# Two-head full attention: four batches in a loop against four batches in one pipeline

## The chip, the cores and the metric

The kernel runs on one core of one Trainium2 chip. The metric is the device time of one execution in microseconds. A core has a matrix engine (TensorE, PE in the profile; its weight loads are PEld), three engines for elementwise work (VectorE or DVE, ScalarE or ACT, GpSimd or POOL) and a queue for transfers (SyncE or SP). Each engine runs its own list of instructions in order; they wait for each other by semaphores. TensorE writes only to PSUM, eight banks of 512 f32 columns on 128 partitions (`ps[:, bank, :]`); GpSimd reads and writes SBUF alone.

## The reference, cut to what matters

The model has two layers over x of 4 batches x 512 rows x 128 columns in f32. Its parts in order: linear attention, windowed attention with a feed-forward part, small-head attention, windowed attention again, small-head mixing, a mixture of experts, then the part that is changed, and a second mixture of experts. The changed part is

```python
x = x + attn_b(_layernorm(x))             # eps 1e-5, no gain

def attn_b(x, ln_gamma, ln_beta, q_gamma, k_gamma, w_q, w_k, w_v, w_o, b_o):
    xn = layernorm(x, ln_gamma, ln_beta)  # a second norm, eps 1e-5
    q, k, v = (heads(xn @ w.T) for w in (w_q, w_k, w_v))   # 2 heads of 64
    qn = rmsnorm(q, q_gamma) * 64 ** -0.5
    kn = rmsnorm(k, k_gamma)
    attn = softmax(einsum('bhid,bhjd->bhij', qn, kn))      # 512 x 512, no mask
    out = merge(einsum('bhij,bhjd->bhid', attn, v))
    return out @ w_o.T + b_o
```

So each row is normed twice in a row, and each head's output goes through its half of the output weights.

## The kernel before, in words

`program` writes one list of instructions for each engine, in eight stages. Between stages every engine drains and counts up `batch_done`; SyncE waits for four of them, clears the semaphores (`clear`, L2109) and counts up `batch_go`, for which all engines wait. The stream x stays in SBUF as `X` (128 partitions x 16 row tiles x 128). The stages up to the fourth are written out in full; the fifth and the seventh are loops (`Fori`).

The seventh stage is `full_attention`, four times, once for each batch (`Fori(0, NB)`, L901, L1275, L1856, L2085). VectorE copies the batch's four row tiles from `X` to `XB` (L1860) and makes two layer norms one after the other (`layer_norm`, L1310): statistics of each tile (L1312), their aggregation (L1315), adding eps (L1317); GpSimd raises to the power -0.5 (`root`, L1879, which also does the 16 columns of q and k later); VectorE subtracts and multiplies (L1320). TensorE turns the result (`transposes`, L318), ScalarE applies gain and offset on the way to `xT` (L1177), and TensorE projects q, k and v: twelve products (L751). Matmuls in f32 appear in the profile as two instructions each, transposes as one. ScalarE squares q and k (L1180) and copies v (L918, the helper for all plain copies); VectorE sums the squares (L1715) and scales (L1716), GpSimd takes the power, VectorE multiplies q and k by it (L1722). TensorE turns both (L318), ScalarE and VectorE copy them out with their gains (L1184, L1725).

Then come four steps, one for each tile of 128 query rows, with both heads in each:

- `scores` (TensorE, L766): 128 x 512 scores for each head, into banks 0 and 1 or 2 and 3 in turn;
- `maxima` (VectorE, L1734 and L1735): the row maximum of both heads, times the negative scale;
- `exps` (ScalarE, L1195): the exponential of each head, with its row sum;
- `turn` (TensorE, L777): eight transposes of the probabilities, into banks 4 and 5;
- the copies out: ScalarE bank 4 (L918), VectorE bank 5 (L1743);
- `values` (TensorE, L786): probabilities times v, eight products of 64 columns, into bank 6.

TensorE's order is scores(0), scores(1), then for each step turn(st), scores(st + 2), values(st). After the fourth step VectorE takes the reciprocal of the sums (L1749) and multiplies (L1750), TensorE turns the result (L318) and multiplies by the output weights (L801), ScalarE copying between, and VectorE adds it and the bias to `XB` (L1754, L1755) and copies back to `X` (L1862). A drain of all engines (`stage_done`, L298) and the hand-over by SyncE end a batch. The eighth stage is `experts(1)`; it begins with the statistics of all 16 tiles of `X`, and in its main loop adds with fused multiply-adds from PSUM (L1805).

Of the kernel before, what the change touches and what calls it, by code (L numbers as in the profile page):

```python
# [111 lines left out]
def program(nc, x_in, w_in, c_in, r_in, out, scratch, c_at):  # L112
# [3 lines left out]
    with ExitStack() as ctx:  # L116
# [35 lines left out]
        def carve(n):  # L152
# [71 lines left out]
        m_qT = carve(512)  # L224
        m_kT = carve(512)
        m_v = carve(512).rearrange("p (j n) -> p j n", j=NT)
        m_p = carve(2048).rearrange("p (z h s) -> p z h s", z=2, h=2)
        m_pT = carve(1024).rearrange("p (h j t) -> p h j t", h=2, j=NT)
        m_os = carve(512)
        m_oT = carve(512)  # L230
        m_sq = carve(1024)
        m_qk = carve(1024).rearrange("p (j n) -> p j n", j=NT)
        m_rs = sb("m_rs", [P, NT * 2])
# [21 lines left out]
            m_xT_ps m_xT m_proj m_sq m_qk_in m_tps m_kT_in m_qv_in m_s m_max m_exp m_tp m_pT_a m_pT_b m_pv  # L255
            m_os_in m_oT_ps m_oT_in m_out""".split()
# [56 lines left out]
        def _(pe):  # L313
# [431 lines left out]
            def full_attention(ln):  # L745
                pe.wait_ge(s.ln_out, ln)
                transposes(0, lambda j: Y[:, j, :]).then_inc(s.m_xT_ps, 1)
                pe.wait_ge(s.m_xT, 1)
                for j in range(NT):
                    for c in range(3):  # L750
                        last = mm(ps[:, 1 + c, j * P:(j + 1) * P], xT[:, j * P:(j + 1) * P],  # L751
                                  W("d_qkv", 128 * c, 128 * c + 128), start=True, stop=True)
                last.then_inc(s.m_proj, 1)
                pe.wait_ge(s.m_qk_in, 1)
                transposes(4, lambda j: m_qk[:, j, 0:128])
                transposes(5, lambda j: m_qk[:, j, 128:256]).then_inc(s.m_tps, 1)
                pe.wait_ge(s.m_qv_in, 1)
                pe.wait_ge(s.m_kT_in, 1)
                steps, dv = full_steps(), DF

                def scores(st):
                    if st >= 2:
                        pe.wait_ge(s.m_exp, st - 1)
                    i, hs = steps[st]
                    for hh, (h, rows) in enumerate(hs):
                        last = mm(ps[:, 2 * (st % 2) + hh, :], m_qT[rows, i * P:(i + 1) * P], m_kT[rows, :],  # L766
                                  start=True, stop=True)
                    last.then_inc(s.m_s, 1)

                def turn(st):  # L770
                    pe.wait_ge(s.m_exp, st + 1)
                    if st:
                        pe.wait_ge(s.m_pT_a, st)
                        pe.wait_ge(s.m_pT_b, st)
                    for hh in range(2):
                        for j in range(NT):
                            last = tr(ps[:, 4 + hh, j * P:(j + 1) * P], m_p[:, st % 2, hh, j * P:(j + 1) * P], ident)  # L777
                    last.then_inc(s.m_tp, 1)

                def values(st):  # L780
                    pe.wait_ge(s.m_pT_a, st + 1)
                    pe.wait_ge(s.m_pT_b, st + 1)
                    i, hs = steps[st]
                    for hh, (h, _) in enumerate(hs):
# [5 lines left out]
                scores(0)  # L790
                scores(1)
                for st in range(len(steps)):
                    turn(st)
                    if st + 2 < len(steps):
                        scores(st + 2)
                    values(st)
                pe.wait_ge(s.m_os_in, 1)
                transposes(0, lambda j: m_os[:, j * P:(j + 1) * P]).then_inc(s.m_oT_ps, 1)
                pe.wait_ge(s.m_oT_in, 1)
                for j in range(NT):  # L800
                    last = mm(ps[:, 1, j * P:(j + 1) * P], m_oT[:, j * P:(j + 1) * P], W("d_wo"), start=True, stop=True)  # L801
                last.then_inc(s.m_out, 1)
# [57 lines left out]
            def stages(which):  # L860
                ln = 0
                for i, st in enumerate(which):
                    if st == "c":
                        ln += 1
                        head_attention(ln)
                    else:
                        ln += 2
                        full_attention(ln)
                    stage_done(pe, i + 1)
# [30 lines left out]
            if STAGES >= 7:  # L900
                with pe.Fori(0, NB) as b:  # L901
                    pe.wait_ge(batch_go, b + NP + 6)
                    pe.sem_inc(batch_seen, 1)
                    stages(["d"])
                    pe.drain().then_inc(batch_done, 1)
            if STAGES >= 8:
                pe.wait_ge(batch_go, NB + NP + 6)
# [7 lines left out]
        def _(act):  # L915
# [259 lines left out]
            def full_attention():  # L1175
                act.wait_ge(s.m_xT_ps, 1)
# [1148 lines left out]
```

## Time and profile before

| | us |
|---|---|
| median of 3 runs | 2269.24 |
| the runs | 2269.24, 2271.3, 2257.24 |
| profiled execution, its own time | 2261.32 |
| its span | 2259.5 |
| TensorE busy (share of the span) | 1630.8 (72%) |
| TensorE weight loads | 1160.5 (51%) |
| VectorE busy | 1318.2 (58%) |
| ScalarE busy | 1083.2 (48%) |
| GpSimd busy | 874.8 (39%) |
| mean granted clock of TensorE | 0.846 |

The span is the stretch that the profile covers, from the first instruction to the last; the execution's own time is 1.8 us longer. Busy shares are means over eight stages. Records give a start, a duration and what ended the idle time before; neighbouring matmuls overlap in their records, so what a group costs is read from start to start. A granted clock of 1.00 is 2.4 GHz, of 0.50 1.2 GHz.

### The profile page before, as it was taken

Reading aid. Unit: us, or ns where it says so; the run is one execution under the profiler, and the core shown is the slowest. Engines: PE = TensorE matmul, PEld = TensorE weight load, DVE = VectorE, ACT = ScalarE, POOL = GpSimd, SP = SyncE. Lnnn points to the kernel's source line nnn. Section 1 sums busy time; section 2 is a strip of 40 time slices with the busy share of each in tenths; the row PEclk is TensorE's granted clock in tenths of the full one; section 3 lists DMA queues with packets and bytes.
Section 4 is the critical chain, followed back from the end, with each engine's and each line's share of the span. In section 5 each row is a group of like instructions: output and inputs, shape, how many; then the busy total and the mean of one; then the engine's idle time right before and its main releaser. Section 6 shows DMA issues by size and latency. Waiting matters only on the chain. (4 is left out here: it accounts for less than half of the span.)

```text
span 2259.5 us, 37774 instructions
## 1 busy us (share of the span) xinstructions
PE 1630.8 (72%) x13344; PEld 1160.5 (51%) x13344; DVE 1318.2 (58%) x3740; ACT 1083.2 (48%) x2727; POOL 874.8 (39%) x628
## 2 busy tenths in 40 slices
PE   6999996889988568988868998884011166455586
PEld 5888883666666333445436666662010055344464
DVE  3454545886776245567568777752968745433344
ACT  3565664877787245654347778762000022222132
POOL 1232234766665013244366666640544402100102
PEclk9999998999999868998779999997555578777578
DMA  4000000111111000000001111100000001000001
GB/s 178 1 1 1 1 1 12 30 27 24 28 30 22 6 0 1 1 1 2 1 20 27 27 26 29 24 20 5 0 0 0 0 1 38 0 0 0 0 4 53
DMA packets 31073, 36.43 MB, mean 16 GB/s; under 512 B 19120, under 2 KB 21168, under 8 KB 30512
## 3 DMA queue, kind: packets, MB, share of 16 engines
q1 hardware_dynamic: 29872, 32.01, 5.4%
q8 instruction: 106, 1.74, 0.3%
q0 software_dynamic: 1024, 2.10, 0.3%
q14 instruction: 71, 0.58, 0.1%
HBM read 12.08 MB, written 3.15 MB: 7 GB/s over the span
## 5 line engine op out<-in xcount | busy, mean ns | idle before, releaser
L918 ACT ACTIVATE arena<-ps 128x512 f32<-128x512 f32 (+5 forms) x684 | 373.8, 606 | 297.9 <-PE ps L318 143.1
L318 PE MATMUL ps<-consts,arena 128*128 128x128 f32 x416 | 89.1, 362 | 296.4 <-DVEq L1695 139.8
L318 PEld LDWEIGHTS ps<-consts,arena 128*128 128x128 f32 x416 | 61.1, 181 | 328.1 <-DVEq L1695 141.6
L1053 ACT ACTIVATE arena<-arena,g_small 128x128 f32<-128x128 f32 x512 | 199.0, 404 | 0.5
L1153 ACT ACTIVATE arena<-ps 128x320 f32<-128x320 f32 (+4 forms) x256 | 132.5, 561 | 137.4 <-PE ps L676 134.6
L1460 DVE CUSTOM_DVE_ANT_0 arena<-ps,consts,g_ss 128x128 f32<-128x128 f32 x512 | 145.6, 347 | 77.1 <-PE ps L482 72.2
L1962 POOL TENSOR_TENSOR arena<-arena,consts 128x512 f32<-128x512 f32 (+1 forms) x64 | 92.9, 1452 | 194.3 <-ACT arena L1153 194.2
L1983 POOL TENSOR_TENSOR arena<-arena 128x512 f32<-128x512 f32 x64 | 82.1, 1282 | 183.8 <-DVE arena L1468 183.7
L2036 POOL TENSOR_TENSOR arena<-arena 128x2048 f32<-128x2048 f32 x16 | 109.5, 6842 | 99.9 <-DVE arena L1687 99.9
L676 PE MATMUL ps<-arena 32*128 32x160 f32 (+4 forms) x1024 | 119.9, 454 | 21.1 <-ACT arena L1153 10.5
L1879 POOL TENSOR_TENSOR rstd<-rstd,consts 128x4 f32<-128x4 f32 (+2 forms) x16 | 28.8, 1798 | 262.4 <-DVE rstd L1317 219.9
L1467 DVE TENSOR_TENSOR arena<-ps,tabs 128x512 f32<-128x512 f32 x128 | 87.7, 685 | 50.7 <-ACT arena L1022 44.8
L1993 POOL TENSOR_TENSOR g_ss<-g_ss,consts 128x8 f32<-128x8 f32 x64 | 105.4, 1647 | 7.1
L1805 DVE SCALAR_TENSOR_TENSOR arena<-ps,arena 128x128 f32<-128x128 f32 x256 | 72.1, 344 | 61.8 <-PE ps L850 60.3
L1402 DVE TENSOR_REDUCE arena<-arena 128x8 f32<-128x1032 f32 x32 | 39.3, 1228 | 115.7 <-ACT arena L976 115.7
L583 PE MATMUL ps<-arena,weights 128*128 128x512 f32 (+1 forms) x192 | 101.4, 639 | 6.0 <-ACT arena L1082 4.1
L676 PEld LDWEIGHTS ps<-arena 32*128 32x128 f32 x1024 | 60.8, 204 | 87.4 <-ACT arena L1153 53.9
L1996 POOL TENSOR_TENSOR g_ss<-g_ss,consts 128x8 f32<-128x8 f32 x64 | 104.7, 1636 | 0.0
L1053 ACT ACTIVATION_READ_ACCUMULATOR arena<-arena,g_small 128x1 f32 x512 | 103.8, 203 | 0.0
L1909 POOL TENSOR_TENSOR arena<-arena,consts 128x8 f32<-128x8 f32 x32 | 52.6, 1645 | 124.2 <-DVE arena L1402 124.2
L2052 POOL DMA_INDIRECT sorted_rows<-arena,e_idx x32 | 30.9, 967 | 169.6 <-DVE arena L1805 162.3
L1986 POOL TENSOR_TENSOR arena<-arena 128x512 f32<-128x512 f32 x64 | 81.4, 1271 | 38.8 <-issue 35.2
(249 smaller groups left out, 4287.2 us busy)
## 6 DMA issues: line engine op xcount, KB each, us to landing
arena<-arena SPq DMA_DIRECT2D x112, 128.0 KB, 2.3
weights<-in_w SPq DMA_DIRECT2D x1, 5069.0 KB, 24.0
weights<-in_w SPq DMA_DIRECT2D x1, 2052.0 KB, 12.5
arena<-Y SPq DMA_DIRECT2D x16, 128.0 KB
arena<-Y SPq DMA_DIRECT2D x16, 127.0 KB
consts<-in_c SPq DMA_DIRECT2D x1, 1278.0 KB, 8.6
out<-X SPq DMA_DIRECT2D x1, 1024.0 KB, 5.1
sorted_rows<-arena,e_idx POOLq DMA_INDIRECT x32
```

What stands on the lines that cost most here:

```text
L318: last = tr(ps[:, bank, j * P:(j + 1) * P], src(j), ident)
L583: mm(ps[0:m, 4 + c % 2, :], W("f_w1", at, at + m), g_hnT, start=True, stop=True)\
L676: last = mm(ps[:, 2 * (st % 2) + hh, 0:n], b_kT[rows, k % 2, r, j * P:(j + 1) * P], b_qT[rows, k % 2, j * P:j * P + n], start=True, stop=True)
L918: copy = lambda o, i: act.activation(o, i, ACT.Copy)
L1053: last = act.activation(g_p[:, n % 2, 4 * hf + i, :], g_sc[:, 4 * hf + i, :], ACT.Exp, scale=-1.0, bias=g_mn[:, h:h + 1], accum_out=g_rs[: ...
L1153: act.activation(b_p[:, U % 2, 2 * gp:2 * gp + 2, at:at + n], ps[:, b:b + 2, 0:n], ACT.Exp, scale=float(HD) ** -0.5).then_inc(s.b_exp, 1)
L1460: last = dve.tensor_tensor_reduce(g_sc[:, 4 * hf + i, :], ps[:, 4 + hf, i * P:(i + 1) * P], C("mask_f" if n % NT else "mask_f0"), g_ss[:, ...
L1467: tt(heads(low[0]), heads(src), table(tabs_at), ALU.mult)
L1962: pool.tensor_tensor(v, v, m.unsqueeze(1).broadcast_to([P, NG, n]), ALU.mult)\
L1993: stepped_after(pool.tensor_tensor(ss[:, 8:16], ss[:, 8:16], C("neghalf", 0, 8), ALU.pow))
L1996: pool.tensor_tensor(ss[:, 0:8], ss[:, 0:8], C("neghalf", 0, 8), ALU.pow).then_inc(gs.root, 1)
L2036: pool.tensor_tensor(c_mix[:, u % 2].rearrange("p (h d t) -> p h d t", h=HB, t=HB), c_e[:, u % 2].unsqueeze(2).broadcast_to(full), vals.un ...
```

## The change

The loop over batches goes; `full_attention` is called once and covers all 16 row tiles. On each engine one loop over a step number t runs from -6 or -4 to 15 or 16. At step t the rows of tile t are worked on, and between them lies one piece of the preparation of a later batch, chosen by (t + 4) % 4 (and (t + 6) % 4 for the norm). `rows_at(t)` is true for t from 0 to 15.

- The two norms are one: the root is taken of v * (1 + eps) + eps * eps instead of v + eps (`norm_var(k, twice)`), and the result goes to `Y` for all batches. The copies between `X` and `XB` go.
- The weights of value and output are multiplied on the chip once at the start (`fold_weights`: one transpose, a copy, a product for each head, a copy). A head's values are then x times a 128 x 128 matrix (`m_w`), so that probabilities times values gives 128 columns for each head, already through the output weights. The output projection with its transposes and copy goes. VectorE adds each head to the stream with a fused multiply-add, scaled by the reciprocal of the head's sum (`add_rows`), and GpSimd adds the bias to `X` (`m_xb`).
- Scores have banks 0 and 1 alone, turned probabilities 2 and 3, values 4, q and k 5 and 6, transposes of x and values 7. The turned x, q, k, the values, the probabilities and the turned probabilities in SBUF have two buffers each.

The core of the diff:

```diff
+            def full_attention():            # TensorE
+
+                def turn_x(z):
+                    pe.wait_ge(gs.ln, 4 * NB + z + 1)
+                    need(pe, s.m_vin, 2 * z)
+                    transposes(7, lambda j: Y[:, NT * z + j, :]).then_inc(s.m_xT_ps, 1)
...
+                def scores(n):
+                    z, i = n // NT, n % NT
+                    pe.wait_ge(s.m_qT, z + 1)
+                    pe.wait_ge(s.m_kT, z + 1)
+                    need(pe, s.m_exp, n)
...
+                def turn_probs(n):
+                    pe.wait_ge(s.m_exp, n + 1)
+                    need(pe, s.m_pT_a, n)
+                    need(pe, s.m_pT_b, n)
...
+                def values(n):
+                    z = n // NT
+                    pe.wait_ge(s.m_pT_a, n + 1)
+                    pe.wait_ge(s.m_pT_b, n + 1)
+                    pe.wait_ge(s.m_vin, 2 * z + 2)
+                    need(pe, s.m_out, n)
+                    for h in range(2):
                         for j in range(NT):
-                            last = mm(ps[:, 6, i * P + h * dv:i * P + (h + 1) * dv], m_pT[:, hh, j, :],
-                                      m_v[:, j, h * dv:(h + 1) * dv], start=j == 0, stop=j == NT - 1)
+                            last = mm(ps[:, 4, h * P:(h + 1) * P], m_pT[:, n % 2, h, j, :], m_v[:, z % 2, h, j, :],
+                                      start=j == 0, stop=j == NT - 1)
...
+                fold_weights()
+                for t in range(-4, TT + 1):
+                    if rows_at(t):
+                        scores(t)
+                    if rows_at(t - 1):
+                        values(t - 1)
+                    z, r = (t + 4) // NT, (t + 4) % NT
+                    if z < NB:
+                        if r == 0:
+                            turn_x(z)
+                        elif r == 1:
+                            project_qk(z)
+                        elif r == 2:
+                            project_v(z, 0)
+                        else:
+                            turn_qk(z)
+                            project_v(z, 1)
+                    if rows_at(t):
+                        turn_probs(t)
```

ScalarE's loop has, in this order at each step, the exponentials of t, the piece (copy of turned x; squares; copy of the first head's values; copies of q and of the second head's values), and the copy of probabilities of head 0. VectorE's loop:

```diff
+                for t in range(-6, TT + 1):
+                    if rows_at(t):
+                        maxima(t)
+                    z, r = (t + 6) // NT, (t + 6) % NT
+                    if z < NB and r == 0:
+                        norm_stats(0, stream(z))
+                        norm_var(0, True)
+                    if z < NB and r == 1:
+                        norm_apply(0, Y[:, NT * z:NT * z + NT, :], stream(z), gs.ln)
+                    z, r = (t + 4) // NT, (t + 4) % NT
+                    if 0 <= z < NB and r == 2:
+                        sums(z)
+                    if rows_at(t - 1):
+                        add_rows(t - 1)
+                    if 0 <= z < NB and r == 2:
+                        normalise(z)
+                    if 0 <= z < NB and r == 3:
+                        keep_k(z)
+                    if rows_at(t):
+                        keep_probs(t)
```

where `sums(z)` reduces the squares and asks GpSimd for the power of 16 columns, `normalise(z)` waits for it and multiplies q and k (two products from PSUM), and `add_rows` is

```diff
+                    dve.wait_ge(s.m_pv, n + 1)
+                    dve.wait_ge(s.m_xb, n // NT + 1)
+                    after(dve.reciprocal(r, r))
+                    stt(x, ps[:, 4, 0:P], r[:, 0:1], x, ALU.mult, ALU.add).then_inc(s.m_half, 1)
+                    dve.wait_ge(s.m_half, n + 1)
+                    stt(x, ps[:, 4, P:2 * P], r[:, 1:2], x, ALU.mult, ALU.add).then_inc(s.m_out, 1)
```

GpSimd's loop has the root of the norm at (t + 6) % 4 == 0, the bias at (t + 6) % 4 == 2, and the power for q and k at (t + 4) % 4 == 2, in this order. The hand-over by SyncE after the stage is kept, once instead of four times.

## Rows read from the trace of the kernel before

**Rows 1.** Windows: from:to, length, busy (instructions) by engine, clock, DMA.

```profile
0.00:1566.20 1566.20, 1322.58 (x11736) 928.22 (x11736) 942.48 (x2917) 956.74 (x2512) 705.61 (x564) 0.92 0.08 20
...
1919.30:1970.70 51.40, 27.26 (x160) 21.07 (x160) 19.98 (x49) 11.42 (x25) 4.95 (x3) 0.73 0.00 0
...
2073.50:2134.80 61.30, 37.24 (x160) 29.10 (x160) 19.88 (x49) 11.53 (x25) 4.91 (x3) 0.58 0.00 0
...
2104.50:2124.90 20.40, 19.52 (x80) 15.57 (x78) 4.70 (x7) 4.56 (x11) 0.00 (x0) 0.50 0.00 0
1950.40:1960.90 10.50, 9.62 (x73) 7.73 (x74) 4.86 (x7) 4.63 (x13) 0.00 (x0) 1.00 0.01 2
```

**Rows 2.** Timeline, first batch ahead of the scores: start, us, instruction, idle before.

```profile
1919.87 0.87 DVE L1312 BATCH_NORM_STATS2 stats<-XB 128x6 f32<-128x128 f32 x4
...
1921.45 1.04 POOL L1879 TENSOR_TENSOR rstd<-rstd,consts 128x4 f32<-128x4 f32 x1 [12.34 <-DVE rstd L1317]
...
1923.67 0.87 DVE L1312 BATCH_NORM_STATS2 stats<-Y 128x6 f32<-128x128 f32 x4
...
1927.46 1.12 PE L318 MATMUL ps<-consts,Y 128*128 128x128 f32 x4 [24.71 <-DVE Y L1320]
...
1929.45 4.97 PE L751 MATMUL ps<-weights,xT 128*128 128x128 f32 x24 [0.87 <-ACT xT L1177]
...
1935.51 1.22 DVE L1715 TENSOR_REDUCE rstd<-arena 128x16 f32<-128x1024 f32 x1 [8.10 <-ACT arena L1180]
...
1939.95 1.29 DVE L1722 TENSOR_TENSOR arena<-ps,rstd 128x512 f32<-128x512 f32 x2 [3.01 <-POOL rstd L1879]
...
1941.29 1.97 PE L318 MATMUL ps<-consts,arena 128*128 128x128 f32 x8 [6.88 <-DVE arena L1722]
...
1944.19 3.54 PE L766 MATMUL ps<-arena 64*128 64x512 f32 x8 [0.94 <-DVE arena L1725]
```

**Rows 3.** Timeline, first batch, its row tiles.

```profile
1947.77 0.69 ACT L1195 ACTIVATE arena<-ps,small 128x512 f32<-128x512 f32 x1 [3.79 <-DVE small L1735]
...
1949.27 1.09 PE L777 MATMUL ps<-consts,arena 128*128 128x128 f32 x8 [1.54 <-ACT arena L1195]
...
1950.30 1.13 PE L766 MATMUL ps<-arena 64*128 64x512 f32 x4
...
1951.36 2.00 PE L786 MATMUL ps<-arena 128*128 128x64 f32 x16
1951.47 1.22 DVE L1734 TENSOR_REDUCE small<-ps 128x2 f32<-128x1024 f32 x1 [0.38 <-PE ps L766]
...
1952.93 0.69 ACT L1195 ACTIVATE arena<-ps,small 128x512 f32<-128x512 f32 x1 [1.77 <-DVE small L1735]
...
1953.19 1.04 PE L777 MATMUL ps<-consts,arena 128*128 128x128 f32 x8
...
1958.14 0.69 DVE L1743 COPY arena<-ps 128x512 f32<-128x512 f32 x1 [1.37 <-PE ps L777]
...
1958.98 1.97 PE L786 MATMUL ps<-arena 128*128 128x64 f32 x16 [0.88 <-DVE arena L1743]
```

**Rows 4.** Timeline, ends of batches: reciprocal, next batch's copy, last copy back.

```profile
1964.71 0.20 DVE L1749 RECIPROCAL m_rs<-m_rs 128x8 f32<-128x8 f32 x1 [2.15 <-PE ps L786]
...
1970.85 0.43 DVE L1860 TENSOR_SCALAR XB<-X 128x512 f32 x1 [0.43 <-SPq L2111]
...
2134.36 0.43 DVE L1862 TENSOR_SCALAR X<-XB 128x512 f32 x1
```

**Rows 5.** Timeline, fourth batch, a step.

```profile
2111.44 2.08 PE L766 MATMUL ps<-arena 64*128 64x512 f32 x4
...
2113.45 3.67 PE L786 MATMUL ps<-arena 128*128 128x64 f32 x16
...
2116.92 1.91 PE L777 MATMUL ps<-consts,arena 128*128 128x128 f32 x8
```

**Rows 6.** Line L1805 by itself: engine, operation, durations in ns, starts, forms.

```profile
L1805 DVE SCALAR_TENSOR_TENSOR arena<-ps,arena x256: 340/343/352, 1849.3 to 2238.6; 128x128 f32<-128x128 f32 x128
```

More of the change, by code:

```diff
@@ L767, in scores @@
                                   start=True, stop=True)
                     last.then_inc(s.m_s, 1)
[L770 to L775, printed above, removed]
+                def turn_probs(n):
+                    pe.wait_ge(s.m_exp, n + 1)
+                    need(pe, s.m_pT_a, n)
+                    need(pe, s.m_pT_b, n)
+                    for h in range(2):
@@ L776, in turn @@
                         for j in range(NT):
-                            last = tr(ps[:, 4 + hh, j * P:(j + 1) * P], m_p[:, st % 2, hh, j * P:(j + 1) * P], ident)
+                            last = tr(ps[:, 2 + h, j * P:(j + 1) * P], m_p[:, n % 2, h, j * P:(j + 1) * P], ident)
                     last.then_inc(s.m_tp, 1)
[L780 to L784, printed above, removed]
+                def values(n):
[4 more added lines that the diff above has]
+                    need(pe, s.m_out, n)
+                    for h in range(2):
@@ L791, in full_attention @@
[L791 to L801, printed above, removed]
@@ L900, in _ @@
             if STAGES >= 7:
[L901 to L905, printed above, removed]
+                pe.wait_ge(batch_go, NP + 6)
+                pe.sem_inc(batch_seen, 1)
+                full_attention()
+                pe.drain().then_inc(batch_done, 1)
             if STAGES >= 8:
-                pe.wait_ge(batch_go, NB + NP + 6)
+                pe.wait_ge(batch_go, NP + 7)
                 pe.sem_inc(batch_seen, 1)
@@ new lines, in exps @@
+                def exps(n):
+                    c = 2 * (n % 2)
+                    act.wait_ge(s.m_max, n + 1)
+                    need(act, s.m_tp, n - 1)
+                    need(act, s.m_out, n - 1)
+                    for h in range(2):
+                        last = act.activation(m_p[:, n % 2, h, :], ps[:, h, :], ACT.Exp, bias=nma[:, c + h:c + h + 1],
+                                              scale=scale, accum_out=m_rs[:, n % 2, h:h + 1])
+                    last.then_inc(s.m_exp, 1)
@@ new lines, in keep_probs @@
+                def keep_probs(n):
+                    act.wait_ge(s.m_tp, n + 1)
+                    need(act, s.m_pv, n - 1)
+                    copy(m_pT[:, n % 2, 0], ps[:, 2, :].rearrange("p (j t) -> p j t", j=NT)).then_inc(s.m_pT_a, 1)
+                act.wait_ge(s.m_wv_ps, 1)
+                copy(m_wv, ps[:, 7, 0:P]).then_inc(s.m_wv, 1)
+                act.wait_ge(s.m_w_ps, 1)
+                copy(m_w, ps[:, 5:7, 0:P]).then_inc(s.m_w, 1)
+                for t in range(-4, TT):
+                    if rows_at(t):
+                        exps(t)
+                    z, r = (t + 4) // NT, (t + 4) % NT
+                    if z < NB:
+                        if r == 0:
+                            keep_x(z)
+                        elif r == 1:
+                            squares(z)
+                        elif r == 2:
+                            keep_values(z, 0)
+                        else:
+                            keep_q(z)
+                            keep_values(z, 1)
+                    if rows_at(t):
+                        keep_probs(t)
@@ L1336, in norm_var @@
                 after(last, True)
-                ts(g_rstd[:, k, :], mv[:, NT * k:NT * k + NT, 1], EPS5, None, ALU.add).then_inc(gs.var, 1)
+                v = mv[:, NT * k:NT * k + NT, 1]
+                if twice:
+                    ts(g_rstd[:, k, :], v, 1.0 + EPS5, EPS5 * EPS5, ALU.mult, ALU.add).then_inc(gs.var, 1)
+                else:
+                    ts(g_rstd[:, k, :], v, EPS5, None, ALU.add).then_inc(gs.var, 1)
                 rooted.next()
@@ L2251, in small_at, with rows_at @@
     return sum(small_width(glob, i) for i in range(j))
-def full_steps():
-    return [(i, [(h, slice(64 * h, 64 * h + 64)) for h in range(2)]) for i in range(NT)]
+def rows_at(n):
+    return 0 <= n < TT
 def kernel(**inputs):
```

272 lines of the change are left out of this document (129 added, 143 removed).

## The prediction

> **What bounds the stage now.** I read the page first (busy shares, the 40 slices, the costliest groups), then the table of windows by stage, then the timeline of one batch. The page spreads the span over eight stages with different limits, so its shares say little here; the change touches only the seventh stage, the two-head attention of the second layer, which the windows place at 1919.4 to 2134.8 us: four batches, one after the other, 51.4 us each in the first three and 61.3 in the fourth [rows 1]. In each of the first three TensorE is busy 27.3 of 51.4 us, VectorE 20, ScalarE 11.4: nobody is full, so the stage is a chain of hand-overs. In the timeline it falls in three parts. Ahead of the scores: two layer norms, projections, q and k normalised, from 1919.41 (the copy L1860, which like that of 1970.85 takes 0.43 us, 0.46 with its hand-over, ahead of the statistics at 1919.87) to 1944.19, where the scores L766 begin: 24.8 us, nearly serial [rows 2, 4]. Then four row tiles, 1944.2 to 1964.71: 20.5 us, where TensorE becomes the bound: one warm step is scores 1.06, values 1.83 and eight transposes 0.98 us, start to start (1950.30, 1951.36, 1953.19), 3.87 together [rows 3]. Then a tail of 6.1 us from the reciprocal (1964.71) to the next batch's copy (1970.85) [rows 4]. The fourth batch costs 9.9 us more with the same instructions: from 2104.5 to 2124.9 TensorE works 19.5 of 20.4 us at a granted clock of 0.50 (1.2 GHz), where a stretch of steps in the first batch had 1.00 (2.4 GHz) [rows 1]. There scores take 2.01, values 3.47 and transposes 1.91: 7.4 us a step [rows 5].
>
> **The stage after, part by part.** Everything is counted from 1919.41, when VectorE may begin.
>
> *Ahead of the first scores.* The copy to XB goes (0.46). One norm instead of two: 1919.87 to 1923.67, 3.80 us; the second (another 3.79 up to 1927.46) goes [rows 2]. Transposes and ScalarE's copy, 1927.46 to 1929.45: 1.99. Query and key projection is 16 of the 24 matmuls of L751: 16/24 of 4.97 is 3.31. From the end of L751 (1934.42) to the reduce at 1935.51: 1.09; from the reduce over the scaling and GpSimd's power of 16 columns to the product at 1939.95: 4.44 (VectorE idle for 3.01 of it); the product to the transposes: 1.34; eight transposes 1.97 [rows 2]. Then PE makes the second head's values (8 instructions at 4.97/24 = 0.207: 1.66) before the scores, while k is scaled. Sum with 0.06 for a hand-over: 19.7 us, where the first batch has 24.8. It is paid once instead of four times: the others' preparation lies in the steps.
>
> *A plain step.* Banks 0 and 1 are the only score banks now, and the PE list of step t is scores(t), values(t-1), a piece of the next batch, transposes(t). The scores of the next step stand behind transposes that wait for both exponentials. So, unlike now, a step is a closed ring: scores to maximum 1.17 (1950.30 to 1951.47), maximum and its scaling to the exponential 1.46 (to 1952.93), two exponentials to the transposes 1.50 (1947.77 to 1949.27), transposes to scores 1.03 (to 1950.30) [rows 3]: 5.16 us. That is longer than the 3.87 of today: this part of the change speaks against it, and costs 16 x 1.29 = 21 us, which the hidden preparation has to earn back. VectorE's adding of rows lies in the ring: a reciprocal, about 0.24, and two fused multiply-adds of 0.343 [rows 4, 6], with hand-overs make 1.02, starting at 2.9 when values end, done by 3.9, ahead of the copy of probabilities at 5.16.
>
> *Steps with a piece.* PE's own sum decides where it passes the ring. Step with transposes of x: 1.06 + 1.83 + 0.5 + 1.0 = 4.4, hidden: 5.16. With the query and key projection (16 matmuls, as values: 1.83): 1.06 + 1.83 + 1.83 + 1.0 = 5.72. With eight transposes of q, k and eight matmuls: 1.2 + 1.83 + 0.95 + 0.92 + 1.0 = 5.9. The fourth kind, with the first head's values, is where VectorE stops everything. Its list there: maximum (done at 1.17 + 1.46 = 2.63), statistics and variance of the norm after (1919.87 to 1921.45: 1.58, so 4.21), sums, add the rows, then the product, which waits for GpSimd's power (4.44 after the sums begin, so 8.65; the rows go into the 3.01 that VectorE idles in it) and takes 1.34 (9.99); only behind it the copy of probabilities (0.69 and a hand-over, 10.72) and the next maximum [rows 2, 3]. A maximum normally starts at 1.17, so this step is 9.55 us; the third such step has no norm any more, 7.97. Queued behind that wait are the copy, so values(t), and the next maximum, so both exponentials: nobody else can fill it.
>
> *Sum of the steps.* Twice 5.16 + 5.72 + 9.55 + 5.9 = 26.33; once 24.75; four plain ones 20.64: 98.05 us. The end after the last transposes: copy 0.84 (1958.14, where the values started at 1958.98), values 1.97 and the rows 1.02: 3.85.
>
> *The clock.* In the long step PE idles from about 6.1 to 10.75, some 4.6 us, and then has cold prices if the clock falls. The rows bound this from both sides: idle stretches of under 1 us between steps keep 1.00 [rows 1, 3], and after the long gaps ahead of the scores the transposes ran at 0.50 (1.97 for eight, not 1.04) [rows 2, 3]. A step of the last kind costs 5.2 us more when all of it is cold (11.1, below, against 5.9); nothing lost is the other end. I take 2.2 for each of three, and 1.5 for the first step, which starts cold: 8 us (0 to 15).
>
> *Edits at nothing.* The product of value and output weights (one transpose, a copy, four matmuls, a copy, 2.3 us by the rows for x) lies under the first norm (3.80), and would cost those 2.3 without it. Values widen from 64 to 128 columns: the same 16 instructions, and cold ones of 128 columns took 0.207 each, those of 64 columns 3.67/16 = 0.229 [rows 2, 5], so width is free; if it doubled the warm 1.83, PE's sum would be 5.7 instead of 5.16 and the stage some 15 us longer; I take 0. The bias moves to GpSimd (idle there); the output projection, its transposes, the division, two adds and the copy back (the 6.1 us tail) go three times outright [rows 4], and the three loop ends in it with them.
>
> **Sum.** 19.7 + 98.05 + 3.85 + 8 = 129.6 us against 215.4 (1919.41 to 2134.79, the end of the last copy back [rows 4]): 85.8 us less. The profiled execution has a span of 2259.5 and a time of 2261.32, so 2175.5 on it. Its time is below the median of the runs (2269.24; 2257.24 to 2271.3); the mean of all four is 2264.8, 3.4 above, so I say **2179 us**. The other stages keep their instructions; their clock may fall differently, a few us either way. A measurement tells about 1% (some 23 us) from no change.
>
> A page rule that speaks against this: the trace shows the eight transposes warm at 1.04 us inside a stretch at 1.00 [rows 1, 3]. The Trainium skill, "TensorE: Matmul & The Clock Gate", Part 4: PE-mode transpose, says that transposes don't count as busy for the clock as matmuls do. By it the gap of the long step is longer for the gate by the transposes in it and all three following steps would be wholly cold (5.2 instead of 2.2 each, 2188 us). No row here separates the two kinds.
>
> **Rivals.**
> (A) *The clock stays at 1.2 GHz through most of the stage*, as in most of the fourth batch, where full work at 0.50 went on for 20 us [rows 1]. The steps are then 2.01 + 3.47 + 1.91 = 7.4 plain, 8.4, 10.8, 9.55 and 11.1 with pieces: 3 x 39.85 + 4 x 7.4 less 0.5 = 148.6; with 19.7 and 6 at the end 174.3, so 41 us less than now: 2224. For it: that row, and the gaps every four steps. Against: three batches in four got 1.00, and a step now has twice the columns in its values and project work between.
> (B) *The long step isn't long*, because the power or the norm costs less in company; then PE's sums set all steps. That takes off 12.8 us of stall and 6.6 of clock: 2160. Against: all in that chain has been taken from rows, and VectorE's list is in order.
> (C) *Slower than now: code supply.* The loop over batches goes and the same work is written out four times. If each PE instruction then had to wait for its code, the stage passes today's 215.4 once 86 us are lost over some 650 PE instructions, 0.13 us each, more than an instruction's own 0.115: a step of some 10.5 us instead of 5.2 to 6. At 0.15 us each it is 97 us: 2276. Against: the first 1566 us are written out likewise and run 11736 matmuls, 7.5 a us, with TensorE busy 1322 us [rows 1]; this stage needs about 5.
> (D) *The change doesn't do what it says*: an unforeseen wait makes batches follow one another again. Four times 19.7 ahead, steps 16 x 5.16, tails of 3: 173, 42 less: 2223. The waits allow batch z+1 to be prepared while z is worked (two buffers each), so little speaks for it.
>
> **Chances.** Forecast 0.77 (its own range 2162 to 2198), A 0.12, B 0.05, D 0.03, C 0.03. The range of 8 in 10 goes from 2160 (B's value, and no clock loss from the fastest run) to 2212 (part of A, or the doubled width and a cold start after each gap). Faster by over 1%: all but C and a rest, 0.96; within 1% 0.01; slower by over 1% 0.03.
>
> **What would show it.** Right: the stage takes 125 to 135 us; the first scores begin 20 us after its start, and the maxima of steps 4 to 16 are about 5.2, 5.7, 9.5 and 5.9 us apart in turn, and 5.2 in the last four; in the long ones VectorE's product waits for the power some 2 us, and TensorE has a gap of 4 to 5 us; the clock shows one dip after each. GpSimd's two kinds of powers and four adds keep their durations. Wrong: plain steps at 7.4 (A), values at over 3 us in a stretch at 1.00 (width), PE gaps put down to issue (C), or no scores while the next batch is projected (D).

## The result, and the profile after

The changed kernel takes 2175.15 us (median of four runs, 2173.67 to 2177.07), the kernel before 2270.27 in the same comparison (2257.24 to 2275.85): a ratio of 0.9601, 95% interval 0.9572 to 0.963, so it is faster by 95 us between the medians and by 4.0% by the ratio. The prediction said 2179, with a range of 2160 to 2212. The profiled execution of the changed kernel takes 2174.38 us with a span of 2172.2; the prediction's sum for a profiled execution was 2175.5. The runs also lie closer together: 3.4 us from lowest to highest, where the kernel before has 18.6. One execution of all those told below, one of the kernel of experiment 2, took 2955.68 us at a mean granted clock of 0.545, and its median and ratio leave it out.

The page of the changed kernel begins:

```profile
span 2172.2 us, 37710 instructions
...
PE 1611.1 (74%) x13333; PEld 1148.2 (53%) x13333; DVE 1305.1 (60%) x3712; ACT 1084.7 (50%) x2729; POOL 875.8 (40%) x628
```

Busy time hardly moved on any engine (TensorE 20 us less, VectorE 13, ScalarE and GpSimd about 1 more). So most of the 87.3 us that the span lost, 68 of them on TensorE, are idle time: nearly the same work now lies side by side. The stage as a window (from:to, length, busy by engine, clock), and its last four steps:

```profile
1920.90:2047.50 126.60, 96.98 (x629) 77.66 (x629) 69.39 (x168) 47.20 (x102) 20.07 (x12) 0.88 0.00 1
2022.90:2047.50 24.60, 18.62 (x129) 13.92 (x128) 13.38 (x28) 8.77 (x21) 0.00 (x0) 1.00 0.00 1
```

TensorE is busy 97 of 126.6 us, where it was 27.3 of 51.4 in a batch [rows 1]; the granted clock is 0.88 on the average of the stage, where batches had 0.73 and 0.58.

The length of the stage is read between two instructions of VectorE: from the end of the update of X by the experts, just ahead of it, to the next stage's first statistics. These are the two of the kernel before, then the two of the changed kernel:

```profile
1916.60 2.29 DVE L1809 TENSOR_TENSOR X<-X,arena 128x2048 f32<-128x2048 f32 x1 [12.50 <-DMA arena<-sorted_rows]
...
2135.13 3.19 DVE L1312 BATCH_NORM_STATS2 stats<-X 128x6 f32<-128x128 f32 x16 [0.34 <-SPq L2111]
```

```profile
1918.22 2.29 DVE L1882 TENSOR_TENSOR X<-X,arena 128x2048 f32<-128x2048 f32 x1 [12.87 <-DMA arena<-sorted_rows]
...
2048.16 3.19 DVE L1360 BATCH_NORM_STATS2 stats<-X 128x6 f32<-128x128 f32 x16 [0.72 <-SPq L2191]
```

The stage had 216.2 us and has 127.6: 88.6 less. The six earlier stages have the same instructions, yet reach this point 1.6 us later (1920.5 against 1918.9), and the last stage is 0.3 shorter: 88.6 - 1.6 + 0.3 = 87.3. These two remainders come and go: in the kernels below, whose first 1900 us are all the same code, the stage began anywhere from 1915.4 to 1926.6. So each experiment is read by the length of its stage first and by its median second.

Ahead of the scores, the timeline of the changed kernel, answering to [rows 2] (start, duration, instruction):

```profile
1920.90 0.87 DVE L1376 BATCH_NORM_STATS2 stats<-X 128x6 f32<-128x128 f32 x4 [0.38 <-SPq L2191]
...
1922.56 0.38 ACT L945 ACTIVATE arena<-ps 128x256 f32<-128x256 f32 x1 [0.90 <-PE ps L752]
...
1924.72 1.11 PE L318 MATMUL ps<-consts,Y 128*128 128x128 f32 x4 [2.21 <-DVE Y L1395]
...
1926.70 3.78 PE L767 MATMUL ps<-weights,arena 128*128 128x128 f32 x16 [0.87 <-ACT arena L1208]
...
1931.58 1.22 DVE L1769 TENSOR_REDUCE m_rn<-arena 128x16 f32<-128x1024 f32 x1 [5.52 <-ACT arena L1214]
...
1936.02 1.29 DVE L1777 TENSOR_TENSOR arena<-ps,m_rn 128x512 f32<-128x512 f32 x2 [3.01 <-POOL m_rn L2126]
...
1940.97 1.51 PE L790 MATMUL ps<-arena 64*128 64x512 f32 x4
```

Statistics to transposes is 3.82 (predicted 3.80), the sums to the product 4.44 (4.44), and the first scores begin 20.07 us after the start (19.7). The second line is the last copy of the multiplied weights: over at 1922.94, 1.8 us before TensorE has its first transposes to do, so hidden as said.

A plain step and the long one, answering to [rows 3]. First the end of a plain step of the last batch, in the same timeline:

```profile
2033.22 1.13 PE L790 MATMUL ps<-arena 64*128 64x512 f32 x4
...
2034.28 2.05 PE L811 MATMUL ps<-arena 128*128 128x128 f32 x16
2034.39 1.23 DVE L1790 TENSOR_REDUCE small<-ps 128x2 f32<-128x1024 f32 x1 [0.38 <-PE ps L790]
...
2035.86 0.69 ACT L1233 ACTIVATE arena<-ps,small 128x512 f32<-128x512 f32 x1 [1.94 <-DVE small L1791]
...
2037.36 1.09 PE L800 MATMUL ps<-consts,arena 128*128 128x128 f32 x8 [1.03 <-ACT arena L1233]
2038.38 1.13 PE L790 MATMUL ps<-arena 64*128 64x512 f32 x4
```

Scores at 2033.22 and at 2038.38: 5.16 us, the ring to the hundredth, and TensorE waits 1.03 of it for the exponentials. The values (L811, now 128 columns wide) take 2.05, where those of 64 columns took 2.00 [rows 3]: the width costs next to nothing here. Then the first long step, VectorE's list and TensorE behind it:

```profile
1954.86 1.23 DVE L1790 TENSOR_REDUCE small<-ps 128x2 f32<-128x1024 f32 x1 [0.38 <-PE ps L790]
...
1956.19 0.86 DVE L1376 BATCH_NORM_STATS2 stats<-X 128x6 f32<-128x128 f32 x4
...
1957.58 1.22 DVE L1769 TENSOR_REDUCE m_rn<-arena 128x16 f32<-128x1024 f32 x1
...
1959.09 2.90 POOL L2126 TENSOR_TENSOR m_rn<-m_rn,consts 128x16 f32<-128x16 f32 x1 [0.32 <-DVE m_rn L1770]
...
1962.02 1.29 DVE L1777 TENSOR_TENSOR arena<-ps,m_rn 128x512 f32<-128x512 f32 x2 [2.17 <-POOL m_rn L2126]
1963.23 0.68 DVE L1796 COPY arena<-ps 128x512 f32<-128x512 f32 x1
1963.83 1.21 DVE L1790 TENSOR_REDUCE small<-ps 128x2 f32<-128x1024 f32 x1
...
1964.01 3.75 PE L811 MATMUL ps<-arena 128*128 128x128 f32 x16 [4.04 <-DVE arena L1796]
```

Maximum to maximum is 8.97; VectorE stands 2.17 us before the product, and the copy behind it keeps TensorE idle for 4.04. When TensorE resumes, the same values take 3.75 instead of 2.05: the clock has fallen. Two windows around that gap and after it show when:

```profile
1958.80:1962.90 4.10, 1.17 (x6) 0.30 (x4) 1.82 (x7) 0.60 (x1) 2.90 (x1) 0.92 0.00 0
1962.90:1969.70 6.80, 5.69 (x29) 5.72 (x30) 4.51 (x12) 2.13 (x5) 1.09 (x1) 0.54 0.00 0
...
1997.00:2047.40 50.40, 41.13 (x299) 32.10 (x297) 28.73 (x58) 20.85 (x47) 2.91 (x1) 1.00 0.00 1
```

### The profile page after: what moved, and what is told of

It reads as the page before. It is cut to its first block and busy times, and to the rows that moved or that the text cites. A ratio compares the mean times of both kernels' runs of the same rounds, so it can differ in the third digit from the quotient of the medians.

```text
span 2172.2 us, 37710 instructions
## 1 busy us (share of the span) xinstructions
PE 1611.1 (74%) x13333; PEld 1148.2 (53%) x13333; DVE 1305.1 (60%) x3712; ACT 1084.7 (50%) x2729; POOL 875.8 (40%) x628
## 5 line engine op out<-in xcount | busy, mean ns | idle before, releaser
L945 ACT ACTIVATE arena<-ps 128x512 f32<-128x512 f32 (+4 forms) x686 | 374.4, 605 | 296.8 <-PE ps L318 126.3
L318 PE MATMUL ps<-consts,arena 128*128 128x128 f32 x400 | 84.4, 358 | 265.9 <-DVEq L1747 139.8
L1454 DVE TENSOR_REDUCE arena<-arena 128x8 f32<-128x1032 f32 x32 | 39.3, 1228 | 115.8 <-ACT arena L1003 115.8
L689 PE MATMUL ps<-arena 128*32 128x160 f32 (+4 forms) x1024 | 87.4, 415 | 4.7 <-issue 4.7
```

The lines of the kernel that those rows point to most:

```text
L318: last = tr(ps[:, bank, j * P:(j + 1) * P], src(j), ident)
L945: copy = lambda o, i: act.activation(o, i, ACT.Copy)
```

## The experiments

The starts of the 16 maxima (L1790, or its line in each kernel) are the ruler: the time between them is the length of a step. Each kernel here has one trace, only the changed one has two, so how far the stage of the kernel before moves from one execution to the next isn't known; a few us of its 216.2 could be of that kind.

**1. The norms alone** (label norm), on the kernel before:

```diff
-                layer_norm(XB[:, 0:NT, :], Y[:, 0:NT, :], NT, EPS5).then_inc(s.ln_out, 1)
-                dve.wait_ge(s.ln_out, 1)
-                layer_norm(Y[:, 0:NT, :], Y[:, 0:NT, :], NT, EPS5).then_inc(s.ln_out, 1)
+                layer_norm(XB[:, 0:NT, :], Y[:, 0:NT, :], NT, EPS5, True).then_inc(s.ln_out, 1)
...
+                if twice:
+                    root(n, ts(rstd[:, 0:n], mv[:, 0:n, 1], 1.0 + EPS5, EPS5 * EPS5, ALU.mult, ALU.add))
```

> The kernel before with one part of the change alone: the two norms made as one, loop over batches and all else as before. If the norms are serial at the head of each batch (the working of the prediction), each of the four batches is shorter by 3.79 us, the stretch from the second statistics to the first transposes: 15 us less, some 2251 to 2256. Rival, that the head was covered by something else: no difference. Second rival, the clock: a batch that starts at another moment may run its row tiles warm or cold, 10 us either way for a batch, as the fourth batch of the kernel before showed.

Measured: 2238.82 against 2257.66 of the kernel before on that chip, ratio 0.9913 (0.9885 to 0.9942). The stage takes 195.4 us, 20.8 less. The batches start

```profile
1915.88 0.43 DVE L1861 TENSOR_SCALAR XB<-X 128x512 f32 x1 [0.52 <-SPq L2111]
...
1963.56 0.43 DVE L1861 TENSOR_SCALAR XB<-X 128x512 f32 x1 [0.43 <-SPq L2111]
...
2011.23 0.43 DVE L1861 TENSOR_SCALAR XB<-X 128x512 f32 x1 [0.45 <-SPq L2111]
...
2060.34 0.43 DVE L1861 TENSOR_SCALAR XB<-X 128x512 f32 x1 [0.44 <-SPq L2111]
```

so the first two take 47.68 and 47.67, 3.8 less than the 51.4 before, as the serial head demands. The third takes 49.1 and the fourth, to the next stage's statistics at 2110.81, 50.5. In the third the row tiles are as long as in the second, and what is longer is the tail behind them, which ran at half the clock. The tails of the second and of the third batch, as windows:

```profile
2005.30:2010.40 5.10, 1.81 (x12) 1.39 (x12) 2.29 (x5) 0.60 (x1) 0.00 (x0) 0.83 0.00 0
2053.00:2059.50 6.50, 3.19 (x12) 2.50 (x12) 2.30 (x5) 0.60 (x1) 0.00 (x0) 0.50 0.00 0
```

The fourth has such a tail too, and its row tiles at 0.79 where the second batch has 0.91, but not the long stretch at 0.50 that made the fourth batch of the kernel before 61.4 us. Serial norms account for 15.2 us; of the 5.6 beyond, the fourth batch gives 7.2 and the third takes back 1.5, both where the granted clock differs.

**2. The weights alone** (fold), on the kernel before, with both norms; the product of the weights is made anew in each batch:

```diff
+                tr(ps[:, 7, 0:P], W("d_qkv", 2 * P, 3 * P), ident).then_inc(s.m_wv_ps, 1)
+                pe.wait_ge(s.m_wv, 1)
+                for h in range(2):
+                    rows = slice(DF * h, DF * h + DF)
+                    last = mm(ps[:, 5 + h, 0:P], m_wv[rows, :], W("d_wo")[rows, :], start=True, stop=True)
...
-                            last = mm(ps[:, 6, i * P + h * dv:i * P + (h + 1) * dv], m_pT[:, hh, j, :],
-                                      m_v[:, j, h * dv:(h + 1) * dv], start=j == 0, stop=j == NT - 1)
+                            last = mm(ps[:, 6 + st % 2, h * P:(h + 1) * P], m_pT[:, h, j, :], m_v[:, h, j, :],
+                                      start=j == 0, stop=j == NT - 1)
...
-                transposes(0, lambda j: m_os[:, j * P:(j + 1) * P]).then_inc(s.m_oT_ps, 1)
```

> The kernel before with the other part alone: value and output weights multiplied on the chip, at the head of each batch under the norms, a head's values 128 columns wide, no division, turning and output projection behind the row tiles, the rows added head by head in the steps, the bias added under the projections; loop over batches and both norms as before. By the rows the tail from the reciprocal to the copy back (5.28 us in the first batch) becomes 1.02, and eight of the 24 projecting matmuls go off the head (1.66): 5.9 us for each batch, 24 in all, some 2242 to 2248. If a product of 128 columns cost twice one of 64, the values would add 1.83 us in each of 16 steps, 29 us, and the kernel would be no faster than before. If the weights' product were not covered, 2.3 us for each batch come back, 9 in all.

Measured: 2231.93 against the same 2257.66, ratio 0.9891 (0.9853 to 0.9929); the stage takes 190.6 us, 25.6 less. The tail, answering to [rows 4]:

```profile
1960.44 0.17 DVE L1753 RECIPROCAL m_rs<-m_rs 128x2 f32<-128x2 f32 x1 [1.32 <-PE ps L798]
1960.64 0.35 DVE L1754 SCALAR_TENSOR_TENSOR XB<-ps,m_rs,XB 128x128 f32<-128x128 f32 x1
1961.03 0.35 DVE L1755 SCALAR_TENSOR_TENSOR XB<-ps,m_rs,XB 128x128 f32<-128x128 f32 x1
1961.52 0.43 DVE L1877 TENSOR_SCALAR X<-XB 128x512 f32 x1
...
1962.38 0.43 DVE L1875 TENSOR_SCALAR XB<-X 128x512 f32 x1 [0.43 <-SPq L2126]
```

From the reciprocal to the copy back is 1.08 us, where it was 5.28 (1964.71 to 1969.99). The wide products cost next to nothing, and their rival of 29 us falls. The 24 us that were expected came out near, but not as four times 5.9. The batches begin

```profile
1916.23 0.43 DVE L1875 TENSOR_SCALAR XB<-X 128x512 f32 x1 [0.52 <-SPq L2126]
...
1962.38 0.43 DVE L1875 TENSOR_SCALAR XB<-X 128x512 f32 x1 [0.43 <-SPq L2126]
...
2010.52 0.43 DVE L1875 TENSOR_SCALAR XB<-X 128x512 f32 x1 [0.45 <-SPq L2126]
...
2058.53 0.43 DVE L1875 TENSOR_SCALAR XB<-X 128x512 f32 x1 [0.44 <-SPq L2126]
```

and the last ends at 2106.33: 46.2, 48.1, 48.0 and 47.8 us. The first is 5.3 shorter than before, the next two 3.3 and 3.4, since a step in each ran mostly at half the clock (0.52 from 1990.0 to 1995.5). The fourth is 13.6 shorter: it has such a step too, but no long stretch at 0.50. Four times 5.3 is 21.2, and the other 4.4 are the clock's.

**3. Both** (normfold), the two edits together.

> Both parts together, still with the loop over four batches. If they add, 39 us less than before, some 2227 to 2232, and what is left to the full change (2175), some 54 us, is the pipeline's alone. If instead the pipeline hides norms and tails anyway and the parts matter little beside it, these 39 us are not additional to what it gives, which shows only in the steps of the changed kernel: there the two parts would have cost room on VectorE and TensorE. Rival by the clock: a batch with less idle time gets 1.00 sooner, and the gain is over 45 us.

Measured: 2220.21 against 2257.66, ratio 0.9829 (0.9802 to 0.9856); the stage takes 173.2 us, 43.1 less. The parts alone gave 20.8 and 25.6, together 3.3 more. In the first batch they add: 42.3 us is 9.1 less than 51.4, and the parts gave 3.8 and 5.3 there. The 3.3 are the clock again: the kernel before has its cold batch to lose only once. So of the stage's 88.6 us the two edits carry 43.1 with the loop kept (some 36 by shorter batches, some 7 by the clock), and the remaining 45.5 (173.2 to 127.6) go with the rest of the change: the pipeline, and with it the loop ends, the copies between `X` and `XB` and the bias on GpSimd, which no run takes apart.

**4. The changed kernel again** (after_again), beside the next three.

> The changed kernel as it is, on the chip and among the runs of the three that follow, so that they can be compared: 2170 to 2177, the stage 127 us, long steps of 8.97, 8.98 and 7.60 us between maxima.

Measured: 2174.78 (2172.57 to 2176.78), ratio 0.9601 (0.9566 to 0.9637); the stage takes 127.7 us, all steps within 0.03 us of the first trace's, the dips of the clock at the same steps.

**5. VectorE's pieces placed elsewhere** (spread), on the changed kernel; GpSimd's root of the norm moves with the statistics:

```diff
+                    z, r = (t + 4) // NT, (t + 4) % NT
+                    if 0 <= z < NB and r == 3:
+                        normalise(z)
-                    z, r = (t + 6) // NT, (t + 6) % NT
+                    z, r = (t + 7) // NT, (t + 7) % NT
                     if z < NB and r == 0:
                         norm_stats(0, stream(z))
                         norm_var(0, True)
-                    if z < NB and r == 1:
+                    if z < NB and r == 2:
...
-                    if 0 <= z < NB and r == 2:
-                        normalise(z)
```

> The changed kernel with VectorE's pieces placed elsewhere, nothing else: norm statistics one step earlier (beside the q and k projection), and the product that waits for GpSimd's power moved behind the maximum of the next step. If the long step is VectorE's in-order wait, as predicted, the third step of a batch falls from 8.97 to 5.2 us; the fourth grows to about 6.9, since the turning of q and k then comes after the product; the gaps of 4 us on TensorE and with them the clock's dips (4.1 us in all in the changed kernel) go: 9 to 12 us less than the changed kernel. Rival: the step is long for another reason (PSUM banks, ScalarE); then the time moves elsewhere and the kernel gains under 3 us.

Measured: 2162.0 against the 2174.78 of after_again, 12.8 us less; ratio to the kernel before 0.9552 (0.9516 to 0.9587). The stage takes 115.8 us, 11.9 less, and its steps are 5.70, 5.16, 6.65 and 5.16 in turn.

```profile
1953.55 1.23 DVE L1790 TENSOR_REDUCE small<-ps 128x2 f32<-128x1024 f32 x1 [0.38 <-PE ps L790]
...
1957.64 0.69 DVE L1796 COPY arena<-ps 128x512 f32<-128x512 f32 x1 [0.48 <-PE ps L800]
1958.71 1.23 DVE L1790 TENSOR_REDUCE small<-ps 128x2 f32<-128x1024 f32 x1 [0.38 <-PE ps L790]
1959.97 0.17 DVE L1791 TENSOR_SCALAR small<-small 128x2 f32<-128x2 f32 x1
1960.05 1.29 DVE L1777 TENSOR_TENSOR arena<-ps,m_rn 128x512 f32<-128x512 f32 x2
```

The copy of probabilities now waits for TensorE, not behind the product, and the product (1960.05) follows the scaling of the maximum with no idle time. No dip of the clock is left after the first step:

```profile
1948.00:2034.00 86.00, 76.32 (x560) 60.60 (x559) 58.45 (x134) 40.29 (x89) 12.94 (x7) 1.00 0.00 1
```

The long step was VectorE's in-order wait.

**6. The order of a step** (ring), on the changed kernel:

```diff
                     if rows_at(t):
                         scores(t)
                     if rows_at(t - 1):
-                        values(t - 1)
+                        turn_probs(t - 1)
+                    if rows_at(t - 2):
+                        values(t - 2)
...
-                    if rows_at(t):
-                        turn_probs(t)
```

> The changed kernel with another order of each step, the long step kept: TensorE gives out the scores of tile t before it turns the probabilities of t - 1 and multiplies those of t - 2; ScalarE and VectorE copy the probabilities of t - 1 ahead of the exponentials and behind the maximum of t; row sums have four buffers. If plain steps are held by the closed ring that includes the transposes (1.17 + 1.46 + 1.50 + 1.03), they fall from 5.16 to 4.15 us, steps with a piece to TensorE's sum: 4.4 and 5.7; some 10 to 14 us less in all, since the long steps hardly move. Rival: TensorE is already the bound in these steps through its weight loads; then a plain step stays over 4.9 and the kernel gains under 4 us.

Measured: 2167.99, 6.8 us less than after_again, and its four runs lie wide (2162.77 to 2173.45); ratio to the kernel before 0.9567 (0.953 to 0.9604). A plain step falls from 5.16 to 4.27 (expected 4.15):

```profile
2027.86 1.22 DVE L1790 TENSOR_REDUCE small<-ps 128x2 f32<-128x1024 f32 x1 [0.52 <-PE ps L790]
...
2032.13 1.22 DVE L1790 TENSOR_REDUCE small<-ps 128x2 f32<-128x1024 f32 x1 [0.52 <-PE ps L790]
```

So the ring did include the transposes, and TensorE was not the bound. But the gain fell short of the expected 10 to 14. The steps together lost 9.3 us; and I had left out that values two steps late put one more of them behind the last maximum: the way from there to the next stage grew from 8.6 to 10.8. The stage: 120.6, 7.1 less.

**7. Both** (full): the order of ring, and on VectorE, at (t + 4) % 4, statistics at 0, the norm at 1, the sums at 2, the product at 3.

```diff
                     if rows_at(t):
                         maxima(t)
+                    if 0 <= z < NB and r == 3:
+                        normalise(z)
+                    if rows_at(t - 1):
+                        keep_probs(t - 1)
+                    if 0 <= z < NB and r == 2:
+                        sums(z)
+                    if z + 1 < NB and r == 0:
+                        norm_stats(0, stream(z + 1))
+                        norm_var(0, True)
+                    if z + 1 < NB and r == 1:
+                        norm_apply(0, Y[:, NT * (z + 1):NT * (z + 1) + NT, :], stream(z + 1), gs.ln)
+                    if rows_at(t - 2):
+                        add_rows(t - 2)
```

> Both: the order of ring, and VectorE's pieces spread, one to a step (norm statistics, norm, sums, product). By the sums of TensorE 4.8, 5.7, 4.8 and 5.9 us in turn and 4.15 in the last four, the stage some 105 us where the changed kernel has 127: 20 to 24 us less than it, 2150 to 2156. If ring and spread only trade the same waits, under 15.

Measured: 2151.28 (2147.47 to 2154.39), 23.5 us less than the changed kernel; ratio to the kernel before 0.9503 (0.9465 to 0.954). The stage takes 108.8 us, 18.9 less; the rest of the 23.5 lies in stages whose code is the same. Steps are 4.3, 5.66, 4.76 and 6.27, plain ones 4.27; the expected 105 is missed by the fourth kind (6.27, not 5.9) and by the longer end that ring had shown. Its row tiles as a window:

```profile
1945.50:2023.00 77.50, 73.76 (x557) 60.16 (x556) 54.66 (x121) 39.76 (x90) 11.91 (x6) 1.00 0.00 1
```

TensorE is busy 73.8 of 77.5 us at full clock: here it is nearly without idle time and so the likely bound (no run tests it), and this version beats both kernels.

**8 and 9. Filling the gap** (fill_mm, fill_tr), on the changed kernel: work for TensorE in its gap behind each long step, whose result nobody reads.

```diff
+                def fill(z):
+                    pe.wait_ge(s.m_vin, 2 * z + 1)
+                    for i in range(18):
+                        mm(ps[:, 7, 0:P], ident, W("d_qkv", 0, P), start=True, stop=True)
...
                     if rows_at(t):
                         scores(t)
+                    if t > 0 and t % NT == NT - 1 and (t + 4) // NT < NB:
+                        fill((t + 4) // NT)
```

and the same with 36 of `tr(ps[:, 7, 0:P], ident, ident)`.

> The changed kernel with 18 products of 128 x 128 (36 matmul instructions, into bank 7, their result overwritten and used by nobody) in TensorE's gap behind each long step, after the scores. They are additional work. If the dips of the clock behind the long steps come from TensorE's gap, the clock holds 1.00 through the row tiles from the first warm stretch on, the fourth steps of the first two batches fall from 8.39 and 7.60 to about 5.95, and the kernel is some 4 us faster with more work in it. If the dips have another cause, they stay and the time is the same or some us longer.

> The same with 36 transposes of the identity instead, which fill the gap for as long. By the clock's showing in the traces so far, nothing tells transposes from matmuls, so the dips go as with the products. If transposes don't count as work for the gate, the dips stay as in the changed kernel (fourth steps of 7.6 to 8.4 us) though TensorE is busy throughout; and slower by the fill where it runs cold (36 x 0.215 = 7.7 us instead of 3.9, some 3.7 us past the gap).

Measured: 2170.45 with products and 2169.78 with transposes, ratios 0.959 (0.9537 to 0.9643) and 0.9587 (0.9535 to 0.9639), which the runs alone can't tell from 0.9601. The traces can: the stages take 125.1 and 125.0 us, 2.7 less, and the fourth steps of the first two batches 5.95 and 5.95 with products, 5.96 and 5.96 with transposes, where they had 8.4 and 7.6. The one behind the third long step, where the gap is shorter (2.66 us) than the added work (4.15), grew from 5.95 to 7.27 and 7.13, so 4.1 gained and 1.3 lost. The gap with transposes, and the row tiles of that kernel:

```profile
1961.99 4.15 PE L818 MATMUL ps<-consts 128*128 128x128 f32 x36
1966.10 2.02 PE L811 MATMUL ps<-arena 128*128 128x128 f32 x16
```

```profile
1960.60:1965.00 4.40, 4.40 (x36) 3.48 (x35) 2.12 (x7) 0.60 (x1) 3.16 (x2) 1.00 0.00 0
...
1951.20:2047.70 96.50, 87.91 (x668) 72.41 (x668) 58.96 (x136) 40.04 (x89) 12.93 (x7) 1.00 0.00 1
```

With either kind of work the clock stays at 1.00 for the whole 96 us behind the first step. So the dips came from TensorE's gap, and 36 f32 transposes in it held the clock as 18 f32 products did.

## Why the prediction was right

The sum was 129.6 us for the stage, from the first work to the end of the last row addition; it measured 126.5 (1920.90 to 2047.44, where the last fused multiply-add of 0.35 us, begun at 2047.09, ends).

- *Ahead of the scores*: 19.7 predicted, 20.07 measured; its stretches came nearly as in [rows 2] (3.82 for 3.80, 4.44 for 4.44).
- *The plain step*: 5.16 predicted, 5.16 measured, and ring showed that the transposes are part of it. The claim that the order of a step works against the change holds: a step of the kernel before took 3.87, this order takes 5.16, and the order of ring 4.27.
- *Steps with a piece*: 5.16, 5.72 and 5.9 predicted; 5.16, 5.70 and 5.95 measured.
- *The long step*: 9.55, 9.55 and 7.97 predicted; 8.97, 8.98 and 7.60 measured. The mechanism was right (spread), the size 0.4 to 0.6 us too large: the pieces of the chain had been taken from rows where the next instruction stands on another engine (maximum to ScalarE 1.46, statistics to GpSimd 1.58, product to TensorE 1.34), or with a hand-over added (copy 0.73). Between neighbours on VectorE, from 1954.86 on, the pieces are 1.33, 1.39, 1.21 and 0.60, each 0.13 to 0.19 shorter; the 4.44 over GpSimd came as predicted. TensorE's gap, predicted at some 4.6 us, was 4.04.
- *The clock*: 8 us predicted (0 to 15), 5.6 measured: 1.46 in the first step, 2.44 and 1.65 behind the first two long steps (gaps of 4.04 and 4.05 us), nothing behind the third (gap of 2.66). The prediction counted three dips. This was a choice between bounds, not a derivation, and that it came near is luck. The fills show the cause of the two dips, the gap; the 1.5 of the first step stays with them.
- *The end*: 3.85 predicted, 3.8 measured (2043.65 to 2047.44).
- *Edits at nothing*: the weights' product was hidden (1.8 us to spare), the width cost next to nothing (2.05 against 2.00), the bias took GpSimd 1.1 us a batch and held nobody.
- *From the profiled execution to the median*: I added 3.4 us since the profiled execution of the kernel before was a low one. That wasn't needed: the changed kernel's runs lie within 3.4 us of each other, and its median is 0.8 above its profiled execution.

Against the sum, the stage measured +0.4 ahead of the scores, -1.5 in the long steps, -2.4 for the clock and some +0.5 in small pieces: 3.1 us shorter. What lies outside the stage, for which the sum has no term, came out 1.9 longer by the executions' own times, so that the profiled execution missed its 2175.5 by only 1.1: part of the closeness is luck.

Of the rivals, A (clock at 1.2 GHz) didn't come: 1.00 from 1997 to 2047. B was wrong: the long step is there, and removing it gave 11.9 us of stage, where B's price was 19.4 for stall and clock together (its 12.8 of stall is 11.6 by the prediction's own terms, 9.55, 9.55 and 7.97 against 5.16). In the changed kernel the stall over 5.16 measured 10.1 and the two dips 4.1, and 2.1 of these 14.2 came back in the three longer fourth steps (6.65 instead of 5.95). C (code supply) and D (batches one after the other) had no experiment; the trace speaks against both. C's sign, a gap of TensorE put down to issue, is there once, the 2.66 us in the third long step, and its values start 0.10 us after VectorE's copy ends (2018.30 and 2018.20), as behind the other two. D's sign, no scores while the next batch is projected, is absent: the projection at 2006.59 stands between the scores at 2003.64 and 2009.35.

The rule of the Trainium skill ("TensorE: Matmul & The Clock Gate", Part 4: PE-mode transpose), that transposes don't count as busy for the clock, would have made all three following steps cold. One of them ran wholly at 1.00, and fill_tr kept 1.00 through a window of 4.4 us with 36 instructions, most of them transposes. For f32 transposes on this chip the measurement decides against it.

What stays open: why the fourth batch of the kernel before ran cold when three equal ones didn't. With the norms or the weights changed, other batches lost part of their warmth, which would fit that it goes with when a batch starts; no run tries this. The wide scatter of the kernel before against the narrow one of the changed kernel would fit, but was not tested either.

## What to carry to other kernels

Serial batches of work that fills no engine can be laid side by side, and here that gave about half (45.5 of 88.6 us, the other half being work saved at the head and tail of each batch). But price each step as a ring: follow the one buffer that has no second copy, and see which instructions of which in-order lists stand between its uses; here the transposes did, and moving them behind the next scores gave 0.9 us in each plain step, 7.1 in the stage. Then put each engine's pieces of preparation on steps of their own, and move an instruction that waits for another engine's answer behind the next thing that everyone else needs: here two such placements were worth 12 us, part of it through TensorE's clock. When a chain is summed from rows, take hand-over times only where the engine changes.

## What I had not expected

Lengthening TensorE's work made the kernel no slower and its stage 2.7 us shorter, by 36 instructions, whose result nobody reads, in a gap of 4 us. And merging norms gave 20.8 us of stage, where the serial count was 15.2: the rest shows as row tiles at a higher clock in the fourth batch (0.79 on their average, where the kernel before had 0.50 for 20.4 us). The first 1900 us, the same code in all these kernels, ended anywhere within 11 us (1915.4 to 1926.6), so a difference of a few us in a median says little about a change unless the stage shows it.
